# Transposing DMAs in place of TensorE transposes ahead of an expert choice, and the choice moved to another place in the step

## What is computed

```python
x = x + attention(layernorm(x), ctx)        # 16 heads of 16, over 512 tokens
r = layernorm(x)
scores = softmax(r @ Wg.T)                  # 8 experts
weights, experts = top_k(scores, 2)
y = sum(gate_e * (W2_e(silu(W1_e r) * W3_e r)) for e in experts)   # each W with a low-rank part
out = x + y
```

## Time and profile before

| | |
|---|---|
| median of 3 runs (lowest, highest) | 1275.65 us (1273.7, 1277.09) |
| the profiled execution: time, span | 1273.23 us, 1271.5 us |
| granted TensorE clock, mean | 0.996 |
| busy share of the span: PE, PEld, DVE, ACT, POOL | 96%, 75%, 81%, 63%, 46% |
| DMA issues of the first stage that the prediction names | `stack<-negmax` x64, 8 KB each, 1.8 us to landing; `stack<-qk_scratch` x256, 128 KB each, 4.8 us |
| norm transposes on TensorE (L757) | x128 |
| scatters (L606) | x128, 1017 ns each on GpSimd |

### The profile page before, as it was taken

The page is one execution under the profiler, slowest core; times in us unless marked ns, Lnnn a source line. Parts: engine busy times, 40 slices in busy tenths (PEclk is TensorE's granted clock), DMA queues, the critical chain, the costliest instruction groups (busy, mean ns, idle before and its releaser), DMA issues.

```text
span 1271.5 us, 34614 instructions
## 1 busy us (share of the span) xinstructions
PE 1223.6 (96%) x11744; PEld 951.6 (75%) x11744; DVE 1024.8 (81%) x3006; ACT 804.5 (63%) x1698; POOL 582.0 (46%) x742
## 2 busy tenths in 40 slices
PE   8899999999999999999998889999999999999997
PEld 6666666666667666766664778888888888888886
DVE  4889999999999999999886776767777767777664
ACT  5378777787777877787667644545555555555443
POOL 6303435554445545454335664444444444444444
PEclk9999999999999999999999999999999999999999
DMA  7777657475665757565466466656675656555554
GB/s 226 139 188 177 125 144 168 125 165 122 156 140 146 151 132 167 125 158 96 116 153 137 148 148 102 93 74 104 103 101 90 104 74 109 83 67 68 67 69 58
DMA packets 179618, 156.33 MB, mean 123 GB/s; under 512 B 105930, under 2 KB 161274, under 8 KB 175354
## 3 DMA queue, kind: packets, MB, share of 16 engines
q1 hardware_dynamic: 153586, 119.29, 44.2%
q0 software_dynamic: 25872, 35.01, 16.4%
HBM read 69.01 MB, written 66.51 MB: 107 GB/s over the span
## 4 chain that ended last, share of the span: by engine, by line
PE 73%; DMA 9%; issue 7%; DVE 4%; POOL 3%; ACT 2%; SPq 1%; POOLq 0%; ACTq 0%; DVEq 0%
PE pv_bank L840 10%; PE st_bank L824 9%; PE s_bank L809 8%; PE bank L83 7%; DMA out_y<-y_out,f_token 7%; PE bank L85 7%; PE bank L84 7%; PE s_bank L83 3%; PE s_bank L84 3%; PE s_bank L85 3%; PE bank L730 3%; POOL f_hold L1562 2%; PE pv_bank L83 1%; PE pv_bank L84 1%; PE st_bank L85 1%
## 5 line engine op out<-in xcount | busy, mean ns | idle before, releaser
L1066 DVE TENSOR_REDUCE maxes<-s_bank 128x2 f32<-128x512 f32 x512 | 345.2, 683 | 56.3 <-PE s_bank L809 50.0
L921 ACT ACTIVATE expo<-st_bank 128x512 f32<-128x512 f32 x512 | 300.5, 597 | 64.2 <-PE st_bank L824 62.2
L1563 POOL DMA_INDIRECT out_y<-y_out,f_token x132 | 206.9, 1567 | 23.6 <-issue 12.9
L824 PE MATMUL st_bank<-stack 67*128 67x256 bf16 x1024 | 196.7, 273 | 3.8 <-ACT expo L921 3.4
L809 PE MATMUL s_bank<-stack 65*128 65x256 bf16 x1024 | 196.2, 272 | 4.0 <-DVE maxes L1066 2.0
L1562 POOL TENSOR_TENSOR f_hold<-ones 128x1 f32<-128x1 f32 x136 | 64.8, 477 | 267.7 <-ACT y_out L1719 260.9
L1719 ACT ACTIVATE y_out<-y_sum,gate 128x256 f32<-128x256 f32 x132 | 59.9, 500 | 153.8 <-DVE y_sum L1842 150.7
L1777 DVE SCALAR_TENSOR_TENSOR vals<-s_bank,b,vals 128x256 f32<-128x256 f32 x146 | 70.3, 483 | 98.4 <-ACT vals L1685 96.5
L83 PE MATMUL s_bank<-xt_hi,stack 128*128 128x256 bf16 x504 | 138.2, 274 | 3.1 <-DVE xt_hi L1759 3.1
L606 POOL DMA_INDIRECT expert_rows<-row,slot x128 | 130.2, 1017 | 21.3 <-issue 20.9
L840 PE MATMUL pv_bank<-expo,vals 128*32 128x256 f32 x2048 | 137.9, 387 | 1.1 <-ACT expo L921 1.1
(11 more groups left out here) (238 smaller groups left out, 3053.2 us busy)
## 6 DMA issues: line engine op xcount, KB each, us to landing
stack<-qk_scratch SPq DMA_DIRECT2D x256, 128.0 KB, 4.8
qk_scratch<-qk SPq DMA_DIRECT2D x32, 512.0 KB, 4.4
x<-in_x SPq DMA_DIRECT2D x16, 512.0 KB, 7.1
ctx_in<-in_ctx SPq DMA_DIRECT2D x16, 512.0 KB, 8.1
out_y<-x SPq DMA_DIRECT2D x32, 256.0 KB, 6.4
expo<-in_w_units SPq DMA_DIRECT2D x18, 256.0 KB
x<-in_w_units SPq DMA_DIRECT2D x18, 256.0 KB
expert_rows<-padding SPq DMA_DIRECT2D x14, 260.0 KB, 3.8
```

The costliest lines, as they stand in the source:

```text
L824: ins = pe.matmul(st_bank[s % 2][:, n, :], stack[k][0:COL_K, 1, h, c * P:(c + 1) * P], stack[k][0:COL_K, 0, h, :], start=True, stop=True)
L921: act.activation(expo[:, s % E_RING], st_bank[s % 2][:], ACT.Exp, scale=SCALE).then_inc(exp_done, 1)
L1066: dve.tensor_reduce(maxes[:, t, h0:h0 + 2], s_bank[r % 2][:], AX_X, ALU.max).then_inc(max_done, 1)
L1563: pool.indirect_dma_start(out=dram["y"], out_offset=bass.IndirectOffsetOnAxis(ap=tokens[turn_of(T)][:, a:a + 1], axis=0), in_=y_outs[turn_ ...
```

## The change

For pieces 0 to 13 (`TURNED = 14`) the rows of the choice are no longer turned by TensorE. The rows' halves, which `split_rows` makes in `row` for the scatter, are turned by four transposing DMAs a piece (128 rows of 512 bf16 each, from SBUF to SBUF) into `rt`, which is now one tile of four blocks. So two `norm` fills a step, with ScalarE's two copies to `rt_hi` and VectorE's two to `rt_lo`, go. The DMAs stand in SyncE's queue behind `unstack` and ahead of the next `stack_max`; they wait for `row_lo_ready` of the piece and for the gate of the piece before.

The choice of piece q-2 (not q-1) is made in step q: `gate` in slot 5, its pieces on VectorE in slots 6 (`shift`), 8 (`pick`) and 10 (`weigh`), ScalarE's exponential in slot 7; `rank` in slot 18 and `assign` in slot 19. All eight scatters of a piece come behind `split_rows`, in slots 20 to 30. Pieces 14 and 15 are chosen as before, so step 15 has the choices of two pieces, 13 and 14. Cut to its core:

```diff
-FILLS = ((3, "sums", -1, 3), (6, "heads", -1, 1), (7, "keys", 2, 0), (8, "out", -1, 1), (9, "max", 0, 1),
+FILLS = ((3, "sums", -1, 3), (5, "gate", -2, 0), (6, "heads", -1, 1), (7, "keys", 2, 0), (8, "out", -1, 1), (9, "max", 0, 1),
...
-         (16, "norm", -1, 0), (17, "norm", -1, 1), (19, "queries", 2, 1), (20, "sums", 0, 1), (22, "gate", -1, 0),
+         (16, "norm", -1, 0), (17, "norm", -1, 1), (18, "rank", -2, 0), (19, "queries", 2, 1), (20, "sums", 0, 1), (22, "gate", -1, 0),
...
-SCATTERS = (7, 10, 16, 18, 21, 24, 26, 29)
-LAST_SCATTERS = (16, 18, 20, 22, 24, 26, 28, 30)
+SCATTERS = (20, 21, 23, 24, 26, 27, 29, 30)
+TURNED = NB - 2
...
+def is_filled(name, p, ahead):
+
+    if not 0 <= p < NB:
+        return False
+    if name == "norm":
+        return p >= TURNED
+    if name in ("gate", "rank"):
+        return p < TURNED if ahead == -2 else p >= TURNED
+    return True
...
-        rt = {h: sb(f"rt_{h}", [P, KC, TOK], BF16) for h in ("hi", "lo")}
+        rt_both = sb("rt", [P, 2 * KC, TOK], BF16)
+        rt = {h: rt_both[:, KC * n:KC * n + KC] for n, h in enumerate(("hi", "lo"))}
...
+        def choosing(q, u, at):
+
+            for ahead, first in ((-2, 5), (-1, 22)):
+                if u == first + at and is_filled("gate", q + ahead, ahead):
+                    return q + ahead
+            return None
...
+            def turn_rows(p):
+
+                if p:
+                    sp.wait_ge(*ready(("gate", p - 1, 0)))
+                sp.wait_ge(row_lo_ready, p + 1)
+                for a in range(TT):
+                    sp.dma_start_transpose(rt_both[:, :, a * P:(a + 1) * P], row_halves[p % 2][:, a, :])\
+                        .then_inc(rt_loaded, 16)
...
                     unstack(q + 2, 0)
+                if 0 <= q - 1 < TURNED:
+                    turn_rows(q - 1)
                 if on(q + 1):
                     stack_max(2 * (q + 1))
...
                     pool.wait_ge(scattered[k], 16 * 2 * TT * (p // 2))
+                    pool.wait_ge(rt_loaded, 16 * TT * (p - 1))
...
-                if 0 <= q - 2 < NB - 3:
-                    slots_known(q - 2)
-                    scatter_at(q - 2, (0, 1))
...
-                    scatter_at(q - 2, range(2, 2 * TT))
+                    slots_known(q - 2)
+                    scatter_at(q - 2, range(2 * TT))
...
             def gate(out, p, n):
-                for c in range(KC):
-                    pe.wait_ge(*free(("norm", p, c)))
+                if p < TURNED:
+                    pe.wait_ge(rt_loaded, 16 * TT * (p + 1))
+                else:
+                    for c in range(KC):
+                        pe.wait_ge(*free(("norm", p, c)))
...
-                    if u == 24 and 0 <= q - 1 < NB:
-                        gate_exp(q - 1)
+                    if choosing(q, u, 2) is not None:
+                        gate_exp(choosing(q, u, 2))
...
-                    if u == 25 and 0 <= q - 1 < NB:
-                        pick(q - 1)
-                    if u == 27 and 0 <= q - 1 < NB:
-                        weigh(q - 1)
+                    if choosing(q, u, 3) is not None:
+                        pick(choosing(q, u, 3))
+                    if choosing(q, u, 5) is not None:
+                        weigh(choosing(q, u, 5))
```

More of the change, by code:

```diff
@@ L63 @@
 STEPS = range(-2, NB + 1)
-FILLS = ((3, "sums", -1, 3), (6, "heads", -1, 1), (7, "keys", 2, 0), (8, "out", -1, 1), (9, "max", 0, 1),
-         (10, "turn", 2, 0), (11, "turn", 2, 1), (12, "keys", 2, 1), (13, "sums", 0, 0), (15, "queries", 2, 0),
-         (16, "norm", -1, 0), (17, "norm", -1, 1), (19, "queries", 2, 1), (20, "sums", 0, 1), (22, "gate", -1, 0),
+FILLS = ((3, "sums", -1, 3), (5, "gate", -2, 0), (6, "heads", -1, 1), (7, "keys", 2, 0), (8, "out", -1, 1), (9, "max", 0, 1),
+         (10, "turn", 2, 0), (11, "turn", 2, 1), (12, "keys", 2, 1), (13, "sums", 0, 0),
+         (15, "queries", 2, 0),
+         (16, "norm", -1, 0), (17, "norm", -1, 1), (18, "rank", -2, 0), (19, "queries", 2, 1), (20, "sums", 0, 1), (22, "gate", -1, 0),
          (23, "heads", 0, 0), (25, "max", 1, 0), (26, "values", 1, 0), (27, "out", 0, 0), (28, "rank", -1, 0),
@@ L94, in plan @@
                 order.append(("bias", 0, 0))
-            order += [(name, q + ahead, n) for s, name, ahead, n in FILLS if s == u and 0 <= q + ahead < NB]
+            order += [(name, q + ahead, n) for s, name, ahead, n in FILLS
+                      if s == u and is_filled(name, q + ahead, ahead)]
     uses, place = [0] * BANKS, {}
@@ L223, in program @@
         row_lo_ready = sem("row_lo_ready")
+        rt_loaded = sem("rt_loaded")
         row_loaded = sem("tile_row_loaded")
@@ L304, in fill_at @@
             name, ahead, n = fills_at[u]
-            return (name, q + ahead, n) if 0 <= q + ahead < NB else None
+            return (name, q + ahead, n) if is_filled(name, q + ahead, ahead) else None
+        def choosing(q, u, at):
[3 more added lines that the diff above has]
+            return None
         def row_slot(q, u):
@@ L640, in _ @@
             for i in range(2 * TT):
-                pool.wait_ge(st_ready, (NB - 1) * SLOTS + LAST_SCATTERS[i] + 1)
+                pool.wait_ge(st_ready, (NB - 1) * SLOTS + SCATTERS[i] + 1)
                 pause(1, i)
@@ L971, in normalize @@
                 if n == "r" and half == 0 and p:
-                    for c in range(KC):
+                    for c in range(KC if p > TURNED else 0):
                         act.wait_ge(*ready(("norm", p - 1, c)))
@@ L1256, in _ @@
                         weights_low(MERGES[u - 4])
-                    if q == NB - 2 and u == 5:
+                    if q == NB - 2 and u == 21:
                         dve.wait_ge(gate_step, (NB - 3) * GATE)
```

## The result

The changed kernel takes 1298.64 us (median of 4 runs, 1294.57 to 1301.03) against 1275.2 for the kernel before in the same comparison (1273.7 to 1277.09): a ratio of 1.0182, 95% interval 1.0157 to 1.0208. It is slower, by 23.4 us. The profiled execution took 1299.07 us, its span is 1297.3 us, 25.8 more than before. The granted clock was 0.986 on the mean, against 0.996 before; in the four runs it was 0.984 to 0.990, the highest in the shortest.

A forecast was written before the change was run, and what follows sets the result against it. TensorE and VectorE, both nearly full, bound the step, VectorE from slot 8 to 25. 17.6 - 2.2 + 1.5 = +16.9 us on the profiled 1273.23 gives 1290.1, with the median 2.4 higher 1292.6 us; range 1281 to 1307.

The forecast's parts named there:

- What moves on VectorE: Shift, pick, weigh and assign, 4.25 us, move to slots 6, 8, 10 and 19; slot 12's row scores wait.
- Slot 8 to slot 25: Row scores of slot 8 to those of slot 25: VectorE's chain sets 22.53 us, 1.44 us more.
- From slot 25 round: Slot 25 to slot 8 of the next step: TensorE sets it, 19.45 us, 0.09 less.
- the 0.33 us of waiting: TensorE's waits for VectorE's maxima in slots 0 and 1, 0.33 us a step, were to go.
- The step: Length of a full step, 2 to 14: 41.98 us, 1.35 more than before.
- The transposes at nothing: Four transposing DMAs a step in SyncE's queue: at most 5.5 us of issue within 7.4 us free, costing nothing.
- Step 1: First step loses its norm fills and has no choice at all: 2.2 us less.
- step 15: Last step has two choices: 1.5 us more, at least 0.96, at most also VectorE's 4.25.
- Thirteen full steps (2 to 14): 13 x 1.35: Steps 2 to 14 each counted as 1.35 us longer, 17.6 us in all.
- Steps 2 to 14 repeat each other: In the kernel before, one step of 40.63 us was taken to stand for all thirteen.
- The first rival: Whole step: VectorE's total decides, each step falls 1.2 us, 16.9 less, 1258.7 us; chance 0.10.

The follow-up runs named there:

- the run with duplicates: Changed kernel with the column scores' matmuls issued two times more in step 14's slots 5 to 26 without a fill; 1296.11 us, ratio 1.0163.
- the one with the late choice: Changed kernel with the choice one step later (gate 22, rank 28), pieces 12 on by the old route, duplicated matmuls in step 14; 1271.99 us, ratio 0.9974.

## Why the prediction was right, and which term was off

The direction and the mechanism hold, and 1298.64 lies within 1281 to 1307, 6 us above the 1292.6 of the forecast. Point by point:

- *What moves on VectorE.* Pick 1.93 (forecast 1.93), weigh 0.71 (0.67), assign 1.12 (1.11). They fell into a stretch without gaps, and the row scores of slot 12 wait: they start 0.89 us behind their column scores, where "about 1 us" was forecast. Slot 8 to slot 25 took 22.57 us (22.53).
- *From slot 25 round.* 19.48 us (19.45). From column to row scores it is 0.22 and 0.32 us in slots 0 and 1, no longer 0.41 and 0.36, so of the 0.33 us of waiting about 0.2 came back, not all.
- *The step.* 42.05 us (41.98).
- *The transposes at nothing.* Right: 5.30 us of issue (at most 5.5), no wait, and the run without them is 1.20 us a step slower than the run with them. But less of the queue was left than forecast: they went out from 331.05 us on, the negated maxima right behind the fourth, and twice the number stops TensorE.
- *Step 1* lost 1.5 us, not 2.2; step 15 and what follows gained 1.3 (1.5).
- **The term that was mis-sized is step 14.** "Thirteen full steps (2 to 14): 13 x 1.35" counts it as a full step, +1.35; it cost 9.4. "Steps 2 to 14 repeat each other" was wrong already of the trace before, where step 14 is 38.61 us and not 40.63, and has waits for VectorE. With the choice moved to slots 6 to 10, VectorE's chain makes TensorE wait 1.3 and 1.6 us at a time there; at full clock that would have been 2.8 us at most by the run with duplicates, and 6.6 or more came from the clock, which the prediction took at 1.00 throughout. This term is 8.1 us of the sum's error. The others agree within 1 us in sum, with step 13 at +0.6 against +1.35: 15.6 + 0.6 - 1.5 + 1.3 + 0.4 = 16.4 measured, 16.9 - 1.35 = 15.5 forecast.

The first rival, that VectorE's total decides, fell most clearly. The changed kernel, the run with gate at slot 2 and the one with the late choice give VectorE 36.70, 36.63 and 36.60 us a step, with the same DMAs, and their steps are 42.05, 41.10 and 40.00 us. The Trainium skill, Perfetto Trace Analysis, section Identifying the Most-Contended Engine, would rank engines by their occupancy and start with the fullest. By it, with VectorE's busy time, these three kernels are alike and all faster than before (37.78 us); the measurement decides, and says that the place of the choice counts for 2 us of the step.

## What to carry to other kernels

Where two engines run in lockstep over two buffers, price a moved piece by the slack of the slots into which it goes, not by the engine's total: the same 3.7 us of choice cost 2.6 us a step more in one place than in another. Look apart at the first and last iterations, in which some of the work is missing: there the engine that was the bound waits, and its clock can halve. And when an edit joins a good part with a bad one, run each alone; here the transposing DMAs were the good one.

## What was not expected of the hardware

**The clock fell without TensorE being idle for long.** In step 14 TensorE was busy 13.30 of the 17.21 us ahead of the fall, with waits of 1.3 to 1.6 us, and was then granted 1.2 GHz for 20.5 of the 23.9 us that followed. It is not the same each time: with the choice moved alone, of steps 2 to 12, with equal slot lengths up to the fall, three fell for 3.4 us and the others did not; and with the same work and waits in step 14 the kernel before kept its clock and the one with pieces 12 and 13 by the old route did not. With waits of 1.4 to 2.8 us at slot 0 (the doubled transposes) it fell in every step from 2 to 14. The Trainium skill, TensorE: Matmul & The Clock Gate, section HAM oscillation — how this bites in real kernels, describes loops that wait for a DMA and fall anew each time; the doubled transposes show that. Step 14, where the waits ahead of the fall were for VectorE, shows a fall without a wait for a DMA.

**A transposing DMA's issue is dear.** One of 128 rows of 512 bf16 from SBUF, 128 KB, takes 1.32 us of SyncE's queue (5.30 for four), as long as one of 256 rows from DRAM (1.37); a plain one of the same 128 KB takes 0.5 in the same queue (eight `stack<-qk_scratch` in 4.00). The Trainium skill, Advanced Engine Details and Errata, section X-Bar Transpose (TRN2), calls transposing DMAs as fast as plain ones. That may hold for the transfer, which no run here shows; for the queue it was over two and a half times as long.
